# Small-head attention layers of a four-layer decoder: the product of probabilities and values moves 64 columns for a head instead of 128

## The reference, cut to what matters

```python
# layer 0, cross-attention (l0x): 32 heads of 8 features, 128 context tokens, rotary positions
# layer 1, self-attention (l1a): 16 query heads in 4 groups, 16 features, causal
scores = jnp.einsum('bhgnd,bhsd->bhns', qg, k) * (1.0 / jnp.sqrt(jnp.float32(d)))
mask = jnp.tril(jnp.ones((T, T), dtype=bool))
att = jax.nn.softmax(jnp.where(mask, scores, -jnp.inf), axis=-1)
y = jnp.einsum('bhns,bhsd->bhnd', att, v)
# layer 2, self-attention (l2a): 16 query heads on 4 key/value heads, 16 features, causal
out = jnp.einsum('bhqk,bhkd->bqhd', attn, v).reshape(b, s, d)
# layer 2, cross-attention (l2x): 16 heads of 16 features; the last 16 of the 128 context
# tokens have their own softmax, and both results are added
def _attn(q, k, v):
    s = jnp.einsum('bhqd,bhkd->bhqk', q, k) * SCALE
    p = jax.nn.softmax(s, axis=-1)
    return jnp.einsum('bhqk,bhkd->bhqd', p, v)
```

## Time and profile before

| | value |
|---|---|
| median of three runs | 3119.93 us (3119.75 to 3129.0) |
| profiled execution, own time | 3125.8 us |
| its span, first to last instruction | 3124.0 us |
| TensorE busy, share of the span | 2754.9 us, 88% |
| VectorE / ScalarE / GpSimd busy | 70% / 61% / 57% |
| `heads_out` (L3619) in l0x, busy | 133.9 us for 1024 records |
| mean granted TensorE clock | 0.945 of full speed |

### The profile page before, as it was taken

The page is one execution under the profiler, slowest core; times in us unless marked ns, Lnnn a source line. Parts: engine busy times, 40 slices in busy tenths (PEclk is TensorE's granted clock), DMA queues, the critical chain, the costliest instruction groups (busy, mean ns, idle before and its releaser), DMA issues. The chain is left out here.

```text
span 3124.0 us, 71366 instructions
## 1 busy us (share of the span) xinstructions
PE 2754.9 (88%) x25227; PEld 2108.8 (68%) x25227; DVE 2192.9 (70%) x5175; ACT 1899.1 (61%) x3885; POOL 1788.9 (57%) x1904
## 2 busy tenths in 40 slices
PE   7969999798999785896788899799999799998998
PEld 5757775466888564674566555688888577776665
DVE  5567764555888523884786677688888587887787
ACT  3346663355777321564786555566666599996675
POOL 2122211223888465653884376699999598987800
PEclk9989999799999876997999999899999999999999
DMA  4010001001333454000001532022212100002000
GB/s 168 1 23 12 14 11 68 7 1 22 72 67 71 155 130 92 6 6 23 16 17 44 229 93 70 16 39 40 38 37 38 21 7 5 5 5 70 2 1 28
DMA packets 230116, 138.31 MB, mean 44 GB/s; under 512 B 175660, under 2 KB 217068, under 8 KB 226927
## 3 DMA queue, kind: packets, MB, share of 16 engines
q1 hardware_dynamic: 225272, 129.67, 15.9%
q0 software_dynamic: 4608, 5.57, 1.1%
HBM read 80.85 MB, written 13.71 MB: 30 GB/s over the span
## 5 line engine op out<-in xcount | busy, mean ns | idle before, releaser
L2238 PE MATMUL bank<-l3a_ln_xnT,far 128*128 128x128 f16 x3072 | 194.2, 220 | 1.8 <-POOL l3a_ln_xnT L2046 1.8
L2238 PEld LDWEIGHTS bank<-l3a_ln_xnT,far 128*128 128x128 f16 x3072 | 181.7, 99 | 17.0 <-POOL l3a_ln_xnT L2046 2.2
L877 PE MATMUL bank<-l2f_xnT,l2f_wi 128*128 128x512 f16 x672 | 157.2, 383 | 7.0 <-POOLq L741 6.4
L3619 PE MATMUL bank<-l0x_v,l0x_pT 128*128 128x128 f32 x1024 | 133.9, 279 | 4.1 <-ACT l0x_pT L4048 2.5
L3619 PEld LDWEIGHTS bank<-l0x_v,l0x_pT 128*128 128x128 f32 x1024 | 126.8, 191 | 14.9 <-issue 5.8
L1226 PE MATMUL bank<-l3f_xnT,near 128*128 128x512 f16 x480 | 120.4, 388 | 6.9 <-DVE l3f_xnT L1011 3.5
L1241 PE MATMUL bank<-near,l3f_h 128*128 128x256 f16 x960 | 119.1, 274 | 5.3 <-DVE l3f_h L1016 2.3
L877 PEld LDWEIGHTS bank<-l2f_xnT,l2f_wi 128*128 128x128 f16 x672 | 65.4, 99 | 78.3 <-POOLq L741 9.9
L1241 PEld LDWEIGHTS bank<-near,l3f_h 128*128 128x128 f16 x960 | 94.1, 98 | 34.5 <-DVE l3f_h L1016 4.0
L3105 ACT ACTIVATE l3x_prob<-bank,l3x_less,l3x_q_rr 128x128 f32<-128x128 f32 x256 | 114.1, 459 | 2.9 <-DVE l3x_less L2984 2.9
L3907 DVE TENSOR_REDUCE l0x_smax<-bank 128x4 f32<-128x512 f32 x128 | 86.3, 686 | 30.4 <-PE bank L3561 28.3
(11 more groups left out here) (733 smaller groups left out, 9298.1 us busy)
## 6 DMA issues: line engine op xcount, KB each, us to landing
far<-in_l1f_in SPq DMA_DIRECT2D x32, 256.0 KB, 3.8
l2f_front<-l2f_shares SPq DMA_DIRECT2D x5, 1024.0 KB, 4.8
sums<-near SPq DMA_DIRECT2D x2, 2176.0 KB, 19.2
far<-in_l1f_down SPq DMA_DIRECT2D x32, 128.0 KB, 4.2
far<-sums SPq DMA_DIRECT2D x8, 512.0 KB, 7.4
l2f_wi<-in_l2f_in SPq DMA_DIRECT2D x14, 256.0 KB, 6.1
far<-l0x_kT SPq DMA_DIRECT2D x64, 48.0 KB
far<-l2x_kT SPq DMA_DIRECT2D x32, 96.0 KB
```

The source lines that it names most:

```text
L877: last = nc.tensor.matmul(bank[:, :], wi16[n % 2][p][:, a, k, :], xnT[q][:, k, 512 * g:512 * g + 512], start=(k + p + q == 0), stop=(k == ...
L2238: last = nc.tensor.matmul(bank[:, P * j:P * j + P], w(k, 512 * c + P * j, P, p), norm.xnT[u][q][:, k, :], start=(k + p + q == 0), stop=(k ...
L3619: last = nc.tensor.matmul(b_o[:, at:at + P], pT[f % 3][:, j, :], v_all[b % NV][:, hv:hv + P], start=True, stop=True)
```

## The change

In `heads_out` both slices become 64 columns wide. The 64 columns still cover the W (at most 34) that are read. `v_all` keeps its width, and no instruction is added, removed or moved on any engine.

```diff
@@ -3616,7 +3616,7 @@
                         h = head(g, u, j)
                         at = W * (h % (H // rounds))
                         hv = W * (h // 4 if kind == "grouped" else h)
-                        last = nc.tensor.matmul(b_o[:, at:at + P], pT[f % 3][:, j, :], v_all[b % NV][:, hv:hv + P],
+                        last = nc.tensor.matmul(b_o[:, at:at + P // 2], pT[f % 3][:, j, :], v_all[b % NV][:, hv:hv + P // 2],
                                                 start=True, stop=True)
                     last.then_inc(o_made, 1)
```

## The result

The changed kernel takes 3176.55 us median of four runs (3173.63 to 3177.76), beside 3121.48 us (3119.75 to 3129.0) of the kernel before in four runs. The ratio is 1.0172, with a 95% interval of 1.0157 to 1.0188: slower by 55 us. The forecast was 3142 us. The profiled execution took 3177.76 us, 52.0 us over that of before.

What follows compares the result with a forecast made beforehand. TensorE was taken to bound l0x, l1a and l2a, sharing l2x's step with VectorE and ScalarE. Terms 0 + 0 + 24, less some 2 us, gave +22 us on the 3119.93 us median: 3142 us, range 3113 to 3178 us.

Steps and rivals of the forecast that it cites:

- Term one: Inside `heads_out` groups: float32 weights set the pace, so halving moved columns saves 0 us; bound 121 us.
- Rival B: Matmuls go by their columns: spacing halves, 121 us of TensorE's time go, 3040 us; chance 0.05.
- Term two: End of a group, before float16 work: next matmul might start 0.055 us earlier; 0 us taken, bound 8 us.
- The sum: All terms together: 0 + 0 + 24, less some 2 us for group ends, +22 us.
- Term three: TensorE's clock in l0x, l1a, l2a and l2x: scattered 5 us lapses to half clock cost 24 us.
- Rival C: l1a falls to the low clock for good: about 40 us, beside 12 to 20 elsewhere, 3175 us; chance 0.13.
- The price of a low stretch: A half-clock stretch of L us loses L x (1 - 0.5 / b), b TensorE's busy share; 0.47 L in l1a.
- the slower case: Whole kernel slower by over 0.3%, chance 0.62 (scattered lapses and C); its own range 3130 to 3160 us.

Runs made afterwards that it cites:

- late_wide: The changed kernel with 128 columns in blocks 8 to 15 of l1a, 64 in blocks 0 to 7; 3158.34 us in one run.
- no_filler: The kernel before (128 columns everywhere) with no filler matmuls in l1a; 3120.54 us in one run.
- the two narrow kernels: The changed kernel (64 columns everywhere) with l1a's filler, 3176.55 us, and the same without that filler, 3155.14 us.
- l1a_96: The changed kernel with 96 moved columns in l1a instead of 64; 3185.25 us in one run.

## Why the prediction was right or wrong

**Term one, 0 us inside a group: right.** The timeline shows the old pace with 64 columns, 0.112 us, and the runs with half the weights show why: load and move overlap and the longer sets the pace. The earlier trace rows with 80 and 32 columns had said it. Rival B was rightly put low.

**Term two, 0 to 8 us at the end of a group: right in size, wrong in place.** Nothing came at the end, where the float16 matmul still starts a full spacing later (1406.24 to 1406.35 us in l2a). The 0.05 us came between the first record and the second. The three parts at full clock have 128 + 64 + 64 pieces; of up to 13 us of TensorE's time l0x and l2a show 1.6 and 2.0 us of length, hardly more than the spread between traces. I had priced a gain at the end alone. The sum took off 2 us for group ends though the term stood at 0.

**Term three, 24 us for the clock: the clock rightly named, the case wrongly chosen, and this is the step that failed.** I took scattered lapses of 5 us in all four parts, 14 of them, for the likeliest, and l1a at half clock throughout for a rival of 0.13. The l1a part of the term, four lapses, stood at 9.4 us; l1a lost 55.1 us, because its clock never rose. Lapses did come in l2x as the theory said, but cost it 1.7 us and not 6; l0x had one and l2a none inside it, where I had 4.5 and 4.6 us. What misled me is the sentence against C: that l1a's projections and mask matmuls can lift the clock at any step. They couldn't, in 16 steps; late_wide shows 89.6 us of a TensorE without idle time at the low clock ahead of its wide products. The earlier trace rows held the fact that counted, that the rise came right behind the first wide product and not in the equally busy 3.4 us before it. The stretch ahead of that one says the same, in the kernel before:

```profile
622.20:625.60 3.40, 3.40 (x19) 1.78 (x17) 2.31 (x6) 2.62 (x7) 1.25 (x3) 0.50 0.00 0
```

From 622.2 to 629.0 us TensorE ran the query projection, the mask matmuls, scores, transposes and filler of l1a without a gap, and the clock stayed low. I should have taken from it that these don't lift the clock there.

Two readings of the prediction don't hold. The filler fills about the last half microsecond up to 629.0 us, not the last one. And narrow float32 work has gone with a rise in the trace before: the low stretch of l1f ends at 1134.2 us, and ahead of it TensorE ran the same three operations (L1920, L1931, L1939) as since 1120.6 us, among them:

```profile
1132.10 1.91 PE L1931 MATMUL bank<-l1f_gT,far 128*128 128x80 f32 x8
1133.80 0.80 PE L1939 MATMUL bank<-far,l1f_eh 128*80 128x256 f32 x2
```

So what the runs show holds for l1a's mix of work, and isn't a rule for every narrow float32 matmul.

**The price of a low stretch.** The busy share gave 81 us for l1a, a guess took half of it, about 40 us; it was 55. In the kernel before, l1a behind the rise reads

```profile
632.50:722.20 89.70, 84.87 (x729) 55.11 (x727) 44.02 (x147) 49.73 (x132) 19.78 (x52) 1.00 0.01 1
```

and about the same work at half clock is the 136.02 us busy of 141.60 above. Busy time grew 1.6 times, and not twice as the formula takes it. At full clock it holds the modelled ends of matmuls and fillers put into idle time: no_filler's l1a is 7 us shorter with TensorE at 77%. How much each counts was not separated. At half clock the same fillers are in the way (22 us between the two narrow kernels).

**The range** of 3113 to 3178 us held the time near its upper end; the slower case's own 3130 to 3160 us did not. Rival C is what happened, but that its 3175 us fits so well is luck: 40 us for l1a were too few (55.1), and the 12 to 20 us for the other parts did not come (together 1.9 us shorter).

The Trainium skill, in "TensorE: Matmul & The Clock Gate" (Why this matters for your kernels), ties the loss of the clock to gaps in which TensorE idles, and its rise to TensorE being kept busy. For the rise the runs don't agree: TensorE was busy 152.50 of 152.50 us in l1a_96 and stayed at 1.2 GHz. The same page's load time by weight columns (LDWEIGHTS) agrees with the pace of 0.112 us at 128 weight columns, and with the fall to 0.65 us for 8 records at 64. It names no clock; at half clock the pace is 0.213 us.

## What to carry to other kernels

Before narrowing a matmul, look at what its weight load costs: here a float32 product on 128 weight columns kept its pace down to 32 moved columns within 7%, so there was next to nothing to win. And look at the row where the clock rises: if it rises right behind the operation to be narrowed, that operation may be the only one that can lift it, and everything to the end of the part may then run at half clock, as l1a did. Rising and holding are two questions; two wide blocks at the start were enough for 14 narrow ones.

## What the runs showed of the hardware that was not expected

- TensorE busy without a gap for 152.5 us in l1a_96 at a granted clock of 0.50, while the kernel with no filler ran at 1.00 with TensorE busy 77%. A full busy column alone doesn't tell the clock.
- Filler matmuls on 128 rows (of the identity matrix) lifted the clock where as many on 64 rows (of weights), with the same moved columns, did not.
- With 128 columns in l1a, and filler on 64 rows or none, the clock rose behind the first product in six traces, behind the second in one and behind the third in one.
- Narrowing the move of float32 groups took some 0.05 us off between the first and the second record of each group and nothing inside or behind it.
- With 64 weight columns and 128 moved ones l0x took 11 us longer than with full weights, at full clock.
